# Scatter-add of the first graph sums: three tables in DRAM in place of four

## The reference, cut to what matters

```python
xw = h6_all @ W
msgs = xw[col_sl] * norm[:, None]
h7 = jax.ops.segment_sum(msgs, row_sl, num_segments=N) + b
h = jax.nn.relu(h7 @ W1 + b1)
out = h @ W2 + b2
```

## Time and profile before

| what | us |
|---|---|
| median of 3 executions | 5548.44 |
| lowest and highest of them | 5533.56, 5564.57 |
| profiled execution, its own time | 5535.18 |
| its span, first to last instruction | 5533.5 |
| scatter stage, first to last POOL scatter | 221.1 to 1088.0 |
| stage after it, first load to last PE and ACT work | 1093.5 to 1204 |

### The profile page before, as it was taken

How to read it: one execution, slowest core, us unless ns; L and a number is a source line. 1 busy time by engine, 2 the same in 40 slices (tenths; PEclk the granted TensorE clock), 3 DMA queues, 4 the chain that set the end, 5 groups by cost and what they waited for, 6 DMA issues and landing times. The chain is left out here.

```text
span 5533.5 us, 69081 instructions
## 1 busy us (share of the span) xinstructions
PE 4208.4 (76%) x19341; PEld 3323.8 (60%) x19341; DVE 3814.4 (69%) x8692; ACT 1622.2 (29%) x3882; POOL 3333.5 (60%) x3108
## 2 busy tenths in 40 slices
PE   4666666377777678887987888798788878878886
PEld 4554445254444566666886666688666667756665
DVE  6644444275555569998436999853699986679998
ACT  3443334230000432222443222234322223422221
POOL 2388888717777467774136777513677750067775
PEclk9888888689999889998998999999899999989998
DMA  4488888736666577786027787612787762077775
GB/s 159 102 123 124 124 122 124 112 118 209 211 212 210 169 236 240 238 242 190 23 73 235 241 244 238 199 32 73 224 245 237 238 188 67 17 220 235 233 239 171
DMA packets 525140, 959.77 MB, mean 173 GB/s; under 512 B 87701, under 2 KB 299875, under 8 KB 523954
## 3 DMA queue, kind: packets, MB, share of 16 engines
q0 software_dynamic: 224512, 549.90, 39.6%
q1 hardware_dynamic: 300130, 404.93, 22.9%
q10 hardware_dynamic: 128, 0.52, 0.0%
HBM read 718.56 MB, written 236.50 MB: 173 GB/s over the span
## 5 line engine op out<-in xcount | busy, mean ns | idle before, releaser
L1462 POOL DMA_INDIRECT L2a_rows<-kv_rows,typed_index x960 | 957.8, 998 | 292.5 <-issue 292.5
L1767 PE MATMUL L2a_sums<-L2a_weighted,L2a_hot 128*128 128x264 f32 x2784 | 791.1, 430 | 204.6 <-DVE L2a_weighted L1617 174.5
L867 POOL DMA_INDIRECT sum_rows<-L0s_rows,L0s_row_of x464 | 726.8, 1566 | 153.7 <-issue 119.3
L1756 PE MATMUL L2a_query<-x,L2a_turned 128*128 x2784 | 727.9, 408 | 50.5 <-ACT L2a_turned L1711 27.8
L1767 PEld LDWEIGHTS L2a_sums<-L2a_weighted,L2a_hot 128*128 128x128 f32 x2784 | 555.3, 209 | 347.8 <-DVE L2a_weighted L1617 199.1
L1756 PEld LDWEIGHTS L2a_query<-x,L2a_turned 128*128 128x128 f32 x2784 | 568.4, 207 | 152.5 <-issue 56.5
L1286 POOL DMA_INDIRECT L1s_rows<-rows,index x464 | 451.1, 972 | 270.4 <-ACTq L87 129.2
L1462 POOL DMA_INDIRECT L3a_rows<-feature_rows,index x464 | 480.9, 1037 | 154.9 <-issue 154.9
L1002 PE MATMUL L0s_message<-features,L0s_share 128*128 x928 | 314.9, 498 | 292.4 <-ACT L0s_share L967 292.4
L1462 POOL DMA_INDIRECT hold<-kv_rows,typed_index x432 | 429.0, 993 | 178.4 <-issue 178.4
L2298 POOL TENSOR_SCALAR L2d_here<-hold,mask 128x256 f32<-128x256 f32 x200 | 183.1, 934 | 537.8 <-DVE hold L2374 389.7
(11 more groups left out here) (428 smaller groups left out, 8319.0 us busy)
## 6 DMA issues: line engine op xcount, KB each, us to landing
code_rows<-L1s_code SPq DMA_DIRECT2D x232, 256.0 KB, 2.9
L3a_code<-code_rows SPq DMA_DIRECT2D x116, 512.0 KB, 4.0
L0s_wide<-source_rows SPq DMA_DIRECT2D x116, 256.0 KB, 3.9
L2a_turn<-turned_rows SPq DMA_DIRECT2D x87, 256.0 KB, 4.4
L2a_pens<-mask_rows SPq DMA_DIRECT2D x87, 256.0 KB
L2a_hot<-hot_rows SPq DMA_DIRECT2D x87, 256.0 KB, 3.9
kv_rows<-L2d_key_rows SPq DMA_DIRECT2D x50, 384.0 KB, 2.6
kv_rows<-L2d_value_rows SPq DMA_DIRECT2D x150, 128.0 KB, 2.4
```

The source lines that it names most:

```text
L867: pool.indirect_dma_start(c.sum_rows[u], bass.IndirectOffsetOnAxis(ap=row_of[:, 4 * n + u:4 * n + u + 1], axis=0), rows[n % ring][:, u, :] ...
L1462: pool.indirect_dma_start(rows[n % ring][:, u, :], None, table, bass.IndirectOffsetOnAxis(ap=index_of[:, t:t + 1], axis=0)).then_inc(lande ...
L1756: last = pe.matmul(query[q % 2][:, u, :], turned[quad % 2][:, u, :], at(c.q, b[2 * q + u // 2]), start=True, stop=True)
L1767: last = pe.matmul(sums[(m * WP + j) % held][:, :], hot[quad % 2][:, j % 2 * 2 + k, :], weighted[:, 2 * j + k, :], start=k == 0, stop=k == 1)
```

## The change

The number of tables goes from four to three. Tile t, counted through all 464, goes to table t mod 3, and POOL waits before its issue for the scatter of tile t - 3 instead of tile t - 4. Three tables are cleared, three loads are issued for each group, and DVE adds three tables and the features with three additions instead of four. `deliver` waits for the same tiles as before, through the new semaphores.

```diff
-KT = 4
+KT = 3
...
                 for u in range(4):
                     if u % 2 == 0:
                         pool.wait_ge(delivered, 2 * n + u // 2 + 1)
-                    wait(pool, added[u], 16 * n)
-                    pool.indirect_dma_start(c.sum_rows[u],
-                                            bass.IndirectOffsetOnAxis(ap=row_of[:, 4 * n + u:4 * n + u + 1], axis=0),
-                                            rows[n % ring][:, u, :], None, compute_op=ALU.add).then_inc(added[u], 16)
+                    t = 4 * n + u
+                    wait(pool, added[t % KT], 16 * (t // KT))
+                    pool.indirect_dma_start(c.sum_rows[t % KT],
+                                            bass.IndirectOffsetOnAxis(ap=row_of[:, t:t + 1], axis=0),
+                                            rows[n % ring][:, u, :], None, compute_op=ALU.add).then_inc(added[t % KT], 16)
...
-                    for k in range(2):
-                        wait(act, added[2 * i + k], 16 * (n - ring + 1))
+                    for t in range(4 * (n - ring) + 2 * i, 4 * (n - ring) + 2 * i + 2):
+                        wait(act, added[t % KT], 16 * (t // KT + 1))
...
-        others = [st.sb(f"other{k}", [P, NB, D])[:, :, :] for k in range(2)]
-        parts = [c.h, c.acc[:, :, 0:D]] + others
+        other = st.sb("other", [P, NB, D])
+        parts = [c.h, c.acc[:, :, 0:D], other[:, :, :]]
...
                 dve.wait_ge(landed[g], 16 * KT)
-                dve.tensor_tensor(others[0][:, own(g), :], others[0][:, own(g), :], others[1][:, own(g), :], ALU.add
-                                  ).then_inc(paired, 1)
-                dve.tensor_tensor(c.h[:, own(g), :], c.h[:, own(g), :], c.acc[:, own(g), 0:D], ALU.add)
-                dve.wait_ge(paired, g + 1)
-                then(dve.tensor_tensor(others[0][:, own(g), :], others[0][:, own(g), :], c.q[:, own(g), 0:D], ALU.add))
-                then(dve.tensor_tensor(c.h[:, own(g), :], c.h[:, own(g), :], others[0][:, own(g), :], ALU.add))
+                dve.tensor_tensor(other[:, own(g), :], other[:, own(g), :], c.q[:, own(g), 0:D], ALU.add)
+                then(dve.tensor_tensor(c.h[:, own(g), :], c.h[:, own(g), :], c.acc[:, own(g), 0:D], ALU.add))
+                then(dve.tensor_tensor(c.h[:, own(g), :], c.h[:, own(g), :], other[:, own(g), :], ALU.add))
```

More of the change, by code:

```diff
@@ L865, in _ @@
                         pool.wait_ge(delivered, 2 * n + u // 2 + 1)
-                    wait(pool, added[u], 16 * n)
-                    pool.indirect_dma_start(c.sum_rows[u],
-                                            bass.IndirectOffsetOnAxis(ap=row_of[:, 4 * n + u:4 * n + u + 1], axis=0),
-                                            rows[n % ring][:, u, :], None, compute_op=ALU.add).then_inc(added[u], 16)
+                    t = 4 * n + u
[3 more added lines that the diff above has]
+                                            rows[n % ring][:, u, :], None, compute_op=ALU.add).then_inc(added[t % KT], 16)
             for k in range(KT):
-                pool.wait_ge(added[k], 16 * quads)
+                pool.wait_ge(added[k], 16 * len(range(k, NT, KT)))
         @block.sync
@@ L1049, in between_sums @@
         landed = [st.sem(f"landed{g}") for g in range(CN)]
-        done, paired, summed, flipped, turned_ready, before_ready, hidden_ready, product_ready, product_free = (
-            st.sem(x) for x in ("done", "paired", "summed", "flipped", "turned_ready", "before_ready", "hidden_ready",
+        done, summed, flipped, turned_ready, before_ready, hidden_ready, product_ready, product_free = (
+            st.sem(x) for x in ("done", "summed", "flipped", "turned_ready", "before_ready", "hidden_ready",
                                 "product_ready", "product_free"))
```

## The result

The changed kernel takes 5571.04 us in the median of 9 runs (5563.93 to 5583.16), the kernel before 5548.44 us in 9 runs beside it. The ratio is 1.0043, 95% interval 1.003 to 1.0057: slower by 23 us. That lies inside the stated range and inside the half per cent that was called no change, but not at the +0.5 us of the sum, and on the side of rival C.

A forecast was written before the change was run, and what follows sets the result against it. POOL's scatters were taken to bound the scatter stage; +8 for waits, -1.9 for loads, -1.4 and -4.2 for additions gave +0.5 us on the median of 5548.44, so 5549 us, range 5530 to 5580.

The forecast's parts named there:

- the sum: All terms of the forecast together: +8 - 1.9 - 1.4 - 4.2 = +0.5 us for the whole kernel.
- rival C: Scatter stage: slot 2 lands 0.5 us later, so slot 1 stalls in every quad; +27 us, 5576; chance 0.15.
- The bound: Scatter stage: POOL, busy 726.80 of 874 us, sets its length; any new wait there reaches the end one for one.
- The wait: POOL's scatters: those landing over 5.45 us after their start delay tile t + 3, mostly from slot 2; +8 us.
- the upper end given: Release after a landing taken as 0.30 us, the gap between scatters paid anew; the wait then costs 16 us.
- The next stage: Stage after the scatters: one load fewer -1.9 us, one addition fewer -1.4 at group 0, -4.2 at groups 2 to 4.
- The rule that was weighed: Scatter landings: 2.0 us plus bytes over 436 GB/s, so no scatter is late; sum -7.5 us; not followed.
- The clearing: Clearing before the scatters: two of eight DMAs go, hidden by PE's and DVE's work of the edge stage; 0 us.
- Else: Semaphores removed, changed addresses in DRAM and freed SBUF: 0 us, no row bears on them.
- B: Scatter stage: no stall, scatters land in time, only the next stage's gains remain; -7.5 us, 5541 to 5536; chance 0.25.
- D: Next stage: no gain, as loads land no sooner and other waits fill PE's stands; +8 us, 5556; chance 0.1.

The follow-up runs named there:

- E2: Kernel before, still scattering to four tables, but the sum takes three and leaves the fourth table's rows out; 5543.04 us, ratio 0.9999.
- E9: Changed kernel (three tables), with SP's 256 KB load issued only after ACT's first copy of messages; 5571.73 us, ratio 1.004.
- E3: Changed kernel (three tables), with DVE's four TENSOR_SCALAR moved ahead of its 128x512 comparison; 5548.22 us, ratio 1.0008.
- E12: Changed kernel (three tables), with DVE's 128x512 comparison of two tensors replaced by four TENSOR_SCALAR of 128x128; 5547.77 us, ratio 1.0002.
- E7: Changed kernel (three tables), with DVE's four TENSOR_SCALAR made SCALAR_TENSOR_TENSOR in the same place; 5568.67 us, ratio 1.0037.
- E14: E12 with the 256 KB load in two halves, the second only after ACT's first copy of messages; 5567.40 us, ratio 1.0042.
- E4: Changed kernel with two tables instead of three, so tile t waits for tile t - 2; 5782.68 us, ratio 1.0434.

## Why the prediction came out as it did

*The bound* was right: POOL's scatters set the scatter stage, and every wait and every lengthening there reached the end of the stage.

*The wait* was the right mechanism at the right slot, and its size was off. Slot 1 waits for slot 2, as told; 45 scatters have a gap over 0.32 us, 35 of them slot 1, where 30 to 60 were forecast. The term was +8 us with 0.1 us of release, from a row read as a wait for ACT. The release after a landing measured 0.27 us, in the middle half of the 45. That is near the upper end given, 0.30, and so is the cost: 15.1 us against that end's 16. With 0.27 in place of 0.1 the landings of before, laid out in the prediction's own way, give 14.7 us, so the release is the term that was mis-sized. That row had been misread. The scatter of 973.99 did not wait for its message, whose copy by ACT had ended at 949.91 us. It waited for the scatter four tiles back, which landed at 972.54, and it started 1.45 us after that. In the kernel before one more scatter waited for a landing, that of the scatter of 787.22, which took 6.85 us (to 794.07); it started 0.73 us later. Its line, and the landing:

```profile
794.80 1.54 POOL L867 DMA_INDIRECT sum_rows<-L0s_rows,L0s_row_of  x1 [0.43 <-issue]
...
DMA to landing us min/median/max: 6.9/6.9/6.9
```

Both are slot 2, and both are over the 0.30 that was taken as the upper end. For slot 1 the kernel before has no such row.

*What was missing:* a moved scatter can be held by DVE. That is the second half of the loss, 17.3 us in POOL's busy time. The row was there to be read: the earlier trace rows has a maximum of 2065 ns beside a median of 1545, and the prediction took 1.54 for all. In the kernel before slot 2 started 0.21 us ahead of the comparison in the median, in the changed one 0.11 us after its start. That the waits at slot 1 cause this shift is argued from their size, 0.3 us where they occur, and from the three runs against three; it was not shown by an experiment of its own, and E2 shows that executions with four tables also come as far as 54 meetings. Nor is it the wait in the same quad alone: of the changed kernel's 65 scatters of slot 2 that lost over 0.15 us, 44 are in quads whose slot 1 had not waited. The Trainium skill, page "SBUF — State Buffer", section "Who interferes with whom", says that a VectorE instruction with two SBUF inputs contends with a GpSimd instruction that reads SBUF. The same page, section "Summary: rules for kernel authors", says that the second of the two to issue is blocked altogether until the first is done. For a scatter that comes second the runs agree: it ends 1.42 us past the comparison's end. But TENSOR_SCALAR with one input tensor hold it too (E9), so the number of inputs tells nothing apart here. The other way round they do not agree: of the 93 comparisons that began during a scatter in the kernel before, none took more than 0.72 us (0.69 alone).

*The next stage*: -7.5 us forecast, -9.9 measured, and -9.7 in E2. The four places were the right ones (the third load, and one addition at groups 0, 2, 3 and 4); PE's stands fell by the 1.4 us counted. The rest is PE's faster work after shorter stands, for which the prediction allowed up to 5 us and counted 0.

*The rule that was weighed*, the fit of the Trainium skill, page "DMA: Bandwidth & Descriptors", section "Anatomy of one DMA — SWDGE (gpsimd) path", would have had no scatter late. Slot 2's median landing of 5.3 us and 15 us of waits show otherwise; a lone scatter's 3.8 us agrees with it.

*The clearing* cost nothing either way: the three stages ahead of the scatters differ by under 1 us. *Else* was put at 0 and left out the 1.9 us between the stages.

In sum: +14.4 waits and +17.3 lengthening, -9.9 in the next stage and 1.9 between the stages give +23.7, against +0.5. The rivals: B did not happen; D did not happen; C's sign came true, but not its mechanism: waits in every quad stayed away, and slot 2's median landing stayed at 5.30 us, under the 5.75 that C needs. That the time lies inside the stated range is therefore luck: the range reached so far up for C's sake, and a dearer release and held scatters took its place.

## What to carry to other kernels

Before a bound queue is given a closer wait, lay the landings out by their place in the loop, not by their median, and add the release of a wait for a DMA: 0.27 us here, and 0.73 where the wait stood in an instruction of its own. Where a group's maximum is far over its median, ask what it met: here a rare 2.06 us became common when the phase moved. Two things helped equally: to move the long DVE instruction away from the scatter's start (E3), and to cut it into short ones (E12), since a scatter is held only for the rest of the one instruction that runs as it starts. Moving a transfer out of one scatter's way put it into the next one's.

## What the runs showed of the hardware that was not expected

- An indirect DMA's issue on POOL that starts while one of DVE's instructions of 128x128 or 128x512 runs, past its first 0.04 to 0.15 us, ends 1.42 us after that instruction's end, instead of 1.54 us after its own start. Beside the TENSOR_TENSOR of 0.69 us it lost up to 0.51 us (changed kernel, 67 of 72 starts held), beside a TENSOR_SCALAR of 0.34 us mostly some 0.08 (E9), beside one of 0.29 us at most 0.09 (E12). Instructions that begin after the issue's start do not hold it (E7).
- The other way round it depends on the form: in the kernel before, TENSOR_TENSOR of 0.69 us that began during a scatter took at most 0.72 us, while single TENSOR_SCALAR took up to 0.63 us, against at most 0.35 outside one.
- The start after a landing: 0.27 us when the scatter instruction itself carried the wait, mostly 0.73 to 0.76 us when the wait stood ahead of it in its own instruction (E9, E14 and E4).
- With two scatters in flight instead of four an undisturbed 128 KB scatter still lands in 3.8 us (slot 0, E4).
